# An R-GCN basis piece comes by one transfer to 120 partitions instead of four to 30 partitions each

## What is computed

```python
def rgcn_gate_layer(x, row, col, edge_type, basis, att, gate_w, root, bias):
    w = jnp.einsum("rb,bio->rio", att, basis)   # basis (30, 512, 512) -> w (2, 512, 512)
    x_j = x[col]
    msgs = []
    for r in range(2):
        gate = jax.nn.sigmoid(x_j @ gate_w[r, :, 0])
        msgs.append(gate[:, None] * x_j @ w[r])
    msg = jnp.where((edge_type == 0)[:, None], msgs[0], msgs[1])
    return jax.ops.segment_sum(msg, row, num_segments=x.shape[0]) + x @ root + bias
...
h = jax.nn.relu(rgcn_gate_layer(x, ..., basis1, att1, ...))
out = rgcn_gate_layer(h, ..., basis2, att2, ...)
```

## Time and profile before

| | |
|---|---|
| time, median of 3 runs | 2426.77 us (2419.44 to 2442.3) |
| the profiled execution | 2415.98 us |
| its span in the profile | 2414.2 us |
| granted TensorE clock, mean | 0.873 |
| TensorE busy | 1881.8 us (78%) |
| VectorE busy | 1392.4 us (58%) |
| GpSimd busy | 954.3 us (40%) |
| ScalarE busy | 428.4 us (18%) |
| HBM read, written | 310.83 MB, 25.10 MB |

### The profile page before, as it was taken

The page is one execution under the profiler, slowest core; times in us unless marked ns, Lnnn a source line. Parts: engine busy times, 40 slices in busy tenths (PEclk is TensorE's granted clock), DMA queues, the critical chain, the costliest instruction groups (busy, mean ns, idle before and its releaser), DMA issues. The chain is left out here.

```text
span 2414.2 us, 32532 instructions
## 1 busy us (share of the span) xinstructions
PE 1881.8 (78%) x7645; PEld 1044.9 (43%) x7646; DVE 1392.4 (58%) x3194; ACT 428.4 (18%) x762; POOL 954.3 (40%) x952
## 2 busy tenths in 40 slices
PE   2777678859899986583688856998697889888984
PEld 1345666644455544472354422333243333443331
DVE  5455768723677756986688765444453444124445
ACT  0112101111455542232000022000161000220000
POOL 0000000010576604400777733777204777017773
PEclk9886569969899997555899978999898999989998
DMA  4992049950566620000576613777415777227775
GB/s 100 218 212 44 0 104 220 214 149 35 169 200 187 187 50 27 0 0 35 157 207 194 185 36 143 205 208 208 84 61 195 210 210 207 57 95 209 209 208 138
DMA packets 99748, 336.65 MB, mean 139 GB/s; under 512 B 19744, under 2 KB 20369, under 8 KB 95851
## 3 DMA queue, kind: packets, MB, share of 16 engines
q0 software_dynamic: 71904, 235.41, 34.7%
q1 hardware_dynamic: 24714, 96.39, 15.3%
q10 hardware_dynamic: 3072, 4.20, 0.9%
HBM read 310.83 MB, written 25.10 MB: 139 GB/s over the span
## 5 line engine op out<-in xcount | busy, mean ns | idle before, releaser
L724 PE MATMUL e_pS<-e_rows,e_onehot_ring 128*128 128x512 f32 x1408 | 693.2, 620 | 158.7 <-issue 44.1
L650 POOL DMA_INDIRECT e_rows<-tab_y,idx_rel x352 | 335.0, 952 | 332.2 <-POOLq L43 122.8
L680 DVE TENSOR_TENSOR acc<-e_pS,acc 128x512 f32 x352 | 242.8, 690 | 379.4 <-PE e_pS L724 377.5
L724 PEld LDWEIGHTS e_pS<-e_rows,e_onehot_ring 128*128 128x128 f32 x1408 | 248.0, 193 | 461.8 <-issue 394.3
L650 POOL DMA_INDIRECT e_rows<-tab_h,idx_h x176 | 188.5, 1071 | 207.7 <-ACTq L616 154.3
L1022 PE MATMUL n_pY<-weights,n_xT_block 128*128 128x512 f32 x560 | 261.6, 618 | 0.0
L773 POOL DMA_INDIRECT e_rows<-tab_q,idx_q x176 | 166.6, 947 | 178.9 <-DVE e_onehot_bf L782 108.6
L650 POOL DMA_INDIRECT e_rows<-tab_n,idx_h x176 | 169.1, 961 | 77.9 <-issue 47.8
L1640 POOL DMA_DIRECT2D a_in<-in_L_gnn_a_src x1 | 1.0, 966 | 496.5 <-POOLq L43 496.5
L846 PE MATMUL e_pS<-e_rows,e_onehot_f 128*128 128x512 f32 x352 | 166.6, 597 | 0.0
L1022 PEld LDWEIGHTS n_pY<-weights,n_xT_block 128*128 128x128 f32 x560 | 108.6, 201 | 119.0 <-issue 119.0
(11 more groups left out here) (290 smaller groups left out, 2757.3 us busy)
## 6 DMA issues: line engine op xcount, KB each, us to landing
basis_piece<-in_L_gnn_basis SPq DMA_DIRECT2D x128, 480.0 KB, 11.8
tab_y<-n_y_ring SPq DMA_DIRECT2D x40, 256.0 KB, 2.2
e_rows<-tab_y,idx_rel POOLq DMA_INDIRECT x352, 3.8
tab_w<-basis_wout ACTq DMA_DIRECT2D x128, 32.0 KB
w_raw<-in_L_gnn_W SPq DMA_DIRECT2D x3, 1024.0 KB, 10.3
weights<-tab_w SPq DMA_DIRECT2D x3, 1024.0 KB, 5.5
e_rows<-tab_q,idx_q POOLq DMA_INDIRECT x176, 3.7
e_rows<-tab_h,idx_h POOLq DMA_INDIRECT x176, 3.8
```

Of the source, the lines that this page charges most:

```text
L650: pool.indirect_dma_start(rows[:, q, s, :], None, table, bass.IndirectOffsetOnAxis(idx[:, j * 2 + s:j * 2 + s + 1], 0)).then_inc(got[q], 16)
L680: nc.vector.tensor_tensor(a, pS[:, u % 4, :], a, ALU.add).then_inc(added, 1)
L724: ins = nc.tensor.matmul(pS[:, u % 4, :], ohr[:, u % 4, s, :], rows[:, u, s, :], start=s == 0, stop=s == 1)
```

## The change

The four transfers of a piece become one: the destination is all 120 partitions of the piece buffer, the source all four chunks of `self.src`. The access pattern of the source walks chunk, then basis, then position (line 170, unchanged), 4 x 30 runs of 4096 numbers, so every number lands where it did. The one transfer adds 16 to loaded[k] instead of 64, and TensorE's wait counts accordingly.

```diff
         def step(i):
             for k in range(2):
                 wait(eng, self.used, (i * 2 + (k - 1)) * 2)
-                for c in range(BCH):
-                    eng.dma_start(self.piece[c * BASES:(c + 1) * BASES, k, :],
-                                  self.src[c, :, bass.ds((i * 2 + k) * BW, BW)]).then_inc(self.loaded[k], 16)
+                eng.dma_start(self.piece[:, k, :], self.src[:, :, bass.ds((i * 2 + k) * BW, BW)]
+                              ).then_inc(self.loaded[k], 16)
         peeled(eng, self.STEPS, step)
...
     def multiply(self, pe, i, k):
 
-        pe.wait_ge(self.loaded[k], (i + 1) * (16 * BCH))
+        pe.wait_ge(self.loaded[k], (i + 1) * 16)
         for s in range(2):
```

## The result

The changed kernel is slower: 2744.35 us median (2730.16 to 2754.61, 4 runs) against 2425.62 us (2419.44 to 2442.3, 4 runs), a ratio of 1.1277 with a 95% interval of 1.1238 to 1.1315. The profiled execution took 2730.16 us, 314.2 us more than the one of before. The forecast was 2923 us; the time lies at the lower edge of the range (2740 to 3200), near the first rival's 2740, and the ratio applied to the profiled execution of before, 2415.98 us, gives 2724.5 us, under that edge. The loss is 314 us where 507 were forecast.

The account below looks back on a forecast made before the run. Basis loads were taken to bound two stretches, 317.8 us together. Four engines at 79.2 GB/s would make them 823 us, +505; with 2 us for the clock, 2415.98 becomes 2923 us, range 2740 to 3200.

Parts of the forecast that it names:

- Rival 1: Basis loads: four engines, each near its best rate of 24.6 GB/s, 320 us a stretch, 2740 us; chance 0.16.
- What bounds the kernel: Two stretches mixing a basis, 317.8 us together, run at the pace of the basis loads; TensorE close behind in the second.
- The number of engines: Merged basis load: largest number up to 16 dividing outer counts 120 and 4, so four engines instead of 15.
- The rate of one engine: Merged basis loads: 19.8 GB/s per engine, 79.2 for four, between bounds of 14.2 and 24.6.
- the thin tail of the basis loads themselves: Last microseconds of each stretch, few engines busy: 17.3 and 17.7 GB/s each, taken as nearest to a four-engine load.
- The sum: Whole kernel: 2415.98 + 505 for the two stretches + 2 for the clock = 2923 us.
- The stores on the four engines: ACT's stores in a stretch: if the loading engines share them, they carry 1.05 MB more, 32.5 MB through four engines.
- The longer wait and the clock: TensorE waits some 17 us a piece for loads; later stages lose nothing, a lower clock at stretch ends costs 2 us.
- The landing time: Sign for the merged basis_piece loads: landing near 50 us, since two stand in the same engines' queues.
- Rival 2: Basis loads keep 15 engines and get wider, 335 GB/s, until TensorE takes over: 2373 us, 1.8% faster; chance 0.04.
- Rival 3: Basis loads keep 15 engines at 216 GB/s, set by the source's rows; 2416 us, nothing changes; chance 0.05.
- Rivals 4 and 5: Basis loads: four engines at the crowded 14.2 GB/s, 3244 us, chance 0.09; one or two engines, over 4000 us, chance 0.02.

## What in the prediction was right, and which step failed

*What bounds the kernel.* Right: both stretches ran at the loads' pace, and 308.2 of the 314.2 us arose there.

*The number of engines.* Right, and the basis of the sign. The count of packets came out as written, 22922, and the one with 15 engines, 23274, came out where the outermost counts, now 120 and 30, were made to share 15. The rule of the Trainium skill's "DMA: Bandwidth & Descriptors", section "Why a DMA increments its semaphore by 16 and not by 1", holds here for unequal counts too: 120 and 4 gave 4 engines, 60 and 2 gave 2.

*The rate of one engine.* This is the step that failed, a term that was mis-sized: 19.8 GB/s taken, 24.5 measured in the middles of the stretches. In the sum's own terms, 32.5 MB in 315.9 us, it was 103 GB/s for four engines in place of 79.2. The forecast leaned on "nearest: the thin tail of the basis loads themselves", with 17.3 at its lower end. That tail was the wrong stand-in, and the trace of before could have said so in two places. Its conclusion, "an engine gets faster as fewer share the work", doesn't fit its own fast bound, where all 16 engines were busy and made 24.6 each. And the tail's windows mix shares; the one microsecond in it with a share near four engines had 100 GB/s:

```profile
488.00:489.00 1.00, 0.99 (x6) 0.60 (x4) 0.07 (x1) 0.00 (x0) 0.00 (x0) 1.00 0.28 100
```

What the runs showed in its place: over a long stretch four engines with transfers queued behind one another settle at the fast end of my bounds, 110 GB/s in all, whether they write 30 partitions apart or next to each other. The 79.2 GB/s weren't far from a real rate: the first 20 us of the first stretch have 77 and 82, and the run with one piece in flight 81 to 83 in its windows. They just don't last. Rival 1 had the price, 320 us a stretch against 315.9 and 310.1 measured, with a chance of 0.16. Its reason, "each engine then reads one chunk by itself", wasn't tested: no run gave four engines another source.

*The sum.* 823 us for the two stretches against 626.0 measured is 197 us too much, all of the difference between 2923 and 2730 but for 4 us on the other side. They are in the later stages, and are less than single runs of one kernel differ by (2419 to 2442 us).

*The stores on the four engines.* Not told apart. With 1.05 MB more, the four engines moved 32.5 MB in 315.9 us, 25.7 GB/s each; without, 24.9.

*The longer wait and the clock.* Right in the main, though TensorE waited 180.6 and 144.6 us for basis_piece and not 250, as the faster loads would have it. Its granted clock fell to 0.67 and 0.76 in the stretches, its work for a piece still fitted, and the end of the second stretch, from the last mix to the next load, took 8.8 us instead of 6.9, the 2 us of the sum.

*The landing time* of basis_piece that I named as a sign isn't in the page of the changed kernel, but the last piece gives it nearly. Its load is issued at 763.3 us, and the mix that waits for it starts at 797.31 us, 34 us later, where I had 50:

```profile
L199 SPq DMA_DIRECT2D basis_piece<-in_L_gnn_basis x32: 630/663/791, 34.8 to 763.3; - x32
```

*Rival 2*, 15 engines and wider, fell in its premise. One transfer over 120 partitions by 15 engines ran at 213 GB/s, like the four narrow ones; the rate rose where each transfer went to every fourth partition, to 252 GB/s. Its price was near the truth for that: 1.8% faster forecast, a ratio of 0.9843 measured, and TensorE does take over in the second stretch.

*Rival 3* fell with the packets, 22922 and not 23274. With 15 engines its price was right, as the run with the basis outermost shows (ratio 0.9997), but its reason was not: source rows side by side gave no gain. *Rivals 4 and 5* fell with the rate and the packets.

Shown is that with 15 engines the destinations change the rate, from 214 to 252 GB/s, that four engines begin slowly and come to 110 GB/s, and that they don't when each piece starts alone. That engines collide, and at memory ports which several partitions share, is a reading for which the Trainium skill gives the map ("SBUF — State Buffer", section "Door 1: The DMA port swizzle": by its map of partitions to ports I estimate that 30 neighbours reach 8 ports, for which its table has about 218 GB/s, and the stretches had 211 to 217, the stores included); no run here looked at a port alone. What keeps 15 engines at 16.6 GB/s each with every fourth partition, why two of four engines were slow when each piece started alone, and why ten engines stayed slow in one stretch and sped up in the next is open.

## What to carry to other kernels

Before merging transfers, look at the outermost count of the source and of the destination as they are written: the number of DMA engines was in every run here the largest number up to 16 that divides both, and a small outer loop (4 chunks) throws away three quarters of them whatever the number of partitions. If the merge is wanted, put the long dimension outermost on both sides. Read the number of engines from the packets of the queue (rows plus one per engine and transfer) and from the DMA share, and when sizing an engine's rate, don't take it from a few microseconds of a tail: the rate of the same engines went from 77 to 110 GB/s within the first 40 us of a stretch.

## What was not expected of the hardware

- The rate of a set of engines depends on its history: the same code gave 77 to 82 GB/s and then 110 (four engines), and 88 and then 166 (ten engines). When each transfer had to wait for the one before, it stayed at 81 to 83 in the windows shown, with two of the four engines done after some 20 us of a piece and two 8 us later.
- Four transfers of 30 rows to every fourth partition moved 252 GB/s where four to neighbours moved 211 to 217; the issue took 812 ns in place of 328.
- A source pitch of 16 KB in place of 1 MB brought no gain at 16 KB a row: 209 and 207 GB/s, for 211 to 217.
